# Two-layer cross-attention on one Trainium2 core: the bias rows of the prediction as two groups of 32 rows, one for each half of the tokens

## What is computed

```python
def _L0_xattn_ref(query, key, Wq, bq, Wk, bk, Wv, bv, Wo, bo):
    Q = jnp.einsum('bqd,dh->bqh', query, Wq) + bq
    K = jnp.einsum('bkd,dh->bkh', key, Wk) + bk
    V = jnp.einsum('bkd,dh->bkh', key, Wv) + bv
    scores = jnp.einsum('bqh,bkh->bqk', Q, K) * HIDDEN_DIM ** -0.5
    weights = jax.nn.softmax(scores, axis=-1)
    attended = jnp.einsum('bqk,bkh->bqh', weights, V)
    return query + jnp.einsum('bqh,hd->bqd', attended, Wo) + bo

def _L1_xattn_ref(emb, latent, Wq, bq, Wk, bk, Wv, bv, gamma, beta):
    q = jnp.einsum('bte,ef->btf', emb, Wq) + bq
    k = jnp.einsum('bml,le->bme', latent, Wk) + bk
    v = jnp.einsum('bml,le->bme', latent, Wv) + bv
    w = jnp.einsum('bte,bme->btm', q, k) / jnp.sqrt(E)
    w = jax.nn.softmax(w, axis=1)
    pred = jnp.einsum('btm,bme->bte', w, v)
    x = pred + emb
    mu, var = jnp.mean(x, -1, keepdims=True), jnp.var(x, -1, keepdims=True)
    return (x - mu) * jax.lax.rsqrt(var + EPS) * gamma + beta

x = _L0_xattn_ref(x, ctx_512, ...)       # x: 64 x 256 x 512, ctx: 64 x 256 x 256
x = _L1_xattn_ref(x, ctx_512, ...)
```

## Times and profile of the kernel before

| | |
|---|---|
| median of three runs | 1355.17 us (1355.1, 1355.17, 1359.16) |
| the profiled execution, its own time | 1356.32 us |
| its span in the profile | 1354.3 us |
| PE matmul busy | 1303.7 us, 96% of the span, 9072 matmuls |
| PE weight load busy | 1198.4 us, 88% |
| DVE, ACT, POOL busy | 837.9 us (62%), 769.2 us (57%), 850.3 us (63%) |
| mean granted TensorE clock | 0.992 |
| DMA | 140.56 MB, 104 GB/s on average |

### The profile page before, as it was taken

The page is one execution under the profiler, slowest core; times in us unless marked ns, Lnnn a source line. Parts: engine busy times, 40 slices in busy tenths (PEclk is TensorE's granted clock), DMA queues, the critical chain, the costliest instruction groups (busy, mean ns, idle before and its releaser), DMA issues.

```text
span 1354.3 us, 25114 instructions
## 1 busy us (share of the span) xinstructions
PE 1303.7 (96%) x9072; PEld 1198.4 (88%) x9072; DVE 837.9 (62%) x1682; ACT 769.2 (57%) x1801; POOL 850.3 (63%) x649
## 2 busy tenths in 40 slices
PE   7999999999999999999999999999999999999994
PEld 5789989998998999999999999999899899989983
DVE  1356666666667566666666666756666666666663
ACT  2356566556655655656655665565565665566542
POOL 3246766666666676676666666667667666666744
PEclk8999999999999999999999999999999999999997
DMA  9013323322322322332232232233233233223011
GB/s 365 17 48 123 110 88 114 116 101 93 124 93 93 124 104 83 122 108 89 112 118 98 93 124 93 93 124 105 83 122 108 89 112 119 98 93 124 34 46 46
DMA packets 29558, 140.56 MB, mean 104 GB/s; under 512 B 3680, under 2 KB 3680, under 8 KB 20960
## 3 DMA queue, kind: packets, MB, share of 16 engines
q1 hardware_dynamic: 28656, 139.47, 28.4%
q10 hardware_dynamic: 880, 0.79, 0.2%
HBM read 106.70 MB, written 33.55 MB: 104 GB/s over the span
## 4 chain that ended last, share of the span: by engine, by line
PE 73%; DVE 13%; ACT 9%; issue 3%; DMA 1%; POOL 0%; ACTq 0%; POOLq 0%; DVEq 0%
PE bank L224 62%; PE bank L230 7%; ACT uT_hi L468 4%; DVE nmax L686 3%; DVE bank L683 3%; DVE PcT_lo L619 3%; DVE uT_lo L626 3%; ACT bank L523 2%; ACT PcT_hi L446 2%; PE bank L355 2%; DMA beta_b<-in_beta 1%; PE bank L371 1%; PE bank L365 1%; DVE yT_lo L619 0%; PE bank L384 0%
## 5 line engine op out<-in xcount | busy, mean ns | idle before, releaser
L836 POOL TENSOR_TENSOR dots<-R,g_b 128x512 f32<-128x512 f32 x128 | 165.0, 1290 | 291.6 <-DVE R L661 275.6
L853 POOL TENSOR_TENSOR Y<-Y,gamma_b 128x512 f32<-128x512 f32 x128 | 165.0, 1291 | 159.0 <-ACT Y L552 159.0
L856 POOL TENSOR_TENSOR Y<-Y,beta_b 128x512 f32<-128x512 f32 x128 | 162.7, 1297 | 0.0
L825 POOL TENSOR_TENSOR xT_lo<-IN,xT_hi 128x1024 fp32r<-128x1024 f32 x64 | 154.2, 2410 | 13.0 <-ACT xT_hi L446 13.0
L224 PE MATMUL bank<-xT_hi,A_hi 128*128 128x256 f32 x512 | 155.8, 304 | 0.0
L828 POOL TENSOR_TENSOR CC_lo<-IN,CC_hi 128x1024 fp32r<-128x1024 f32 x64 | 153.9, 2405 | 0.0
L446 ACT ACTIVATE yT_hi<-bank 128x512 fp32r<-128x512 f32 x128 | 69.6, 596 | 141.5 <-PE bank L230 141.5
L224 PE MATMUL bank<-xT_hi,A_lo 128*128 128x256 f32 x512 | 145.1, 283 | 0.0
L224 PE MATMUL bank<-xT_lo,A_hi 128*128 128x256 f32 x512 | 144.5, 282 | 0.0
L661 DVE SCALAR_TENSOR_TENSOR R<-bank,rz,R 128x512 f32<-128x512 f32 x128 | 96.0, 751 | 77.6 <-PE bank L224 77.6
L224 PE MATMUL bank<-yT_hi,A_hi 128*128 128x256 f32 x512 | 143.5, 280 | 0.5 <-DVE yT_lo L619 0.2
(11 more groups left out here) (117 smaller groups left out, 4254.6 us busy)
## 6 DMA issues: line engine op xcount, KB each, us to landing
IN<-in_packed SPq DMA_DIRECT2D x64, 1024.0 KB, 4.8
R<-in_x SPq DMA_DIRECT2D x64, 512.0 KB, 3.3
out<-Y SPq DMA_DIRECT2D x64, 512.0 KB, 2.6
WqT_s<-in_WqT SPq DMA_DIRECT2D x2, 1024.0 KB, 11.2
WkT_s<-in_WkT SPq DMA_DIRECT2D x2, 512.0 KB, 12.2
Wo_s<-in_Wo SPq DMA_DIRECT2D x1, 1024.0 KB, 12.7
WvT_s<-in_WvT SPq DMA_DIRECT2D x1, 512.0 KB, 10.4
Wv_s<-in_Wv SPq DMA_DIRECT2D x1, 512.0 KB, 20.6
```

What stands on the lines that cost most here:

```text
L825: nc.gpsimd.tensor_tensor(flat(xT[n.k % 2][1]), raw[:, 0:XW], fp(flat(xT[n.k % 2][0])), ALU.subtract).then_inc(xT_lo, 1)
L836: nc.gpsimd.tensor_tensor(dots[q][:, :], R[n.k % 4][:, q, :], g1_b[:, :], ALU.mult).then_inc(dot_set, 1)
L853: nc.gpsimd.tensor_tensor(y[:, q, :], y[:, q, :], gamma_b[:, :], ALU.mult).then_inc(Y_mul, 1)
L856: last = nc.gpsimd.tensor_tensor(y[:, q, :], y[:, q, :], beta_b[:, :], ALU.add)
```

## The change

The matmul of 128 rows at the head of each half is gone. In its place each half has a group of five rows in 32 partitions: half 0 in partitions 0 to 31, half 1 in partitions 32 to 63. Two matmuls of 32 contraction rows and 512 columns, one into bank 6 and one into bank 7, stand next to each other in the new function `biases(n)` at the end of PE's body, behind the product of half 1. `pred_full` is now counted by them. The products start their banks themselves.

`pick` has ones in columns 0 to 2 and 32 to 34. A small table `marks`, loaded from memory, makes the five rows of a group: `s_h` writes `s_top`, the rounded sum of `s_bank` and a mark, over 64 rows, and `s_l` writes `srow` as `s_top` times a mark plus `s_bank`, over 64 rows, in place of a subtraction on one row. The rows of a group hold high, low and high of `s`, and two ones; `bvK` holds the same five products as before. On DVE `x2(r-1, 0)` leaves its place and stands directly ahead of `x2(r-2, 1)` at the head of the next body. The small loads are ten in place of seven: one for the marks, four for the rows of `bv1` and `bo0` (10 rows of 2 KB in all, in place of 128), and the rest as before.

```diff
-        bvK = sb("bvK", [P, D], f32r)
-        row = sb("row", [P, D])
-        row_hi = sb("row_hi", [P, D], f32r)
-        less = sb("less", [P, 1])
+        bvK = sb("bvK", [2 * 32, D], f32r)
+        row = sb("row", [2 * 32, D])
+        row_hi = sb("row_hi", [2 * 32, D], f32r)
+        mark = sb("mark", [P, 3])
...
-        srow = sb("srow", [P, S], f32r)
+        s_top = sb("s_top", [2 * 32, S], f32r)
+        srow = sb("srow", [2 * 32, S], f32r)
...
         def _(pe):
-            def product(dst, stat, mov, k, first=True):
+            def product(dst, stat, mov, k, stop=True):
                 for t in range(k):
                     for n, (a, b) in enumerate(((0, 0), (0, 1), (1, 0))):
-                        last = nc.tensor.matmul(dst, stat(a, t), mov(b, t), start=(first and t == 0 and n == 0),
-                                                stop=(t == k - 1 and n == 2))
+                        last = nc.tensor.matmul(dst, stat(a, t), mov(b, t), start=(t == 0 and n == 0),
+                                                stop=(stop and t == k - 1 and n == 2))
                 return last
...
                     pe.wait_ge(x2_set, n.count(2, q, back=1))
-                dst = pred_bank[q][:, :]
-                nc.tensor.matmul(dst, srow[:, q * P:(q + 1) * P], bvK[:, :], start=True, stop=False)
-                product(dst, lambda a, t: wcT[a][:, t, q * P:(q + 1) * P], lambda b, t: V1[b][:, t, :], LT,
-                        first=False).then_inc(pred_full, 1)
+                product(pred_bank[q][:, :], lambda a, t: wcT[a][:, t, q * P:(q + 1) * P], lambda b, t: V1[b][:, t, :], LT,
+                        stop=False)
+
+            def biases(n):
+                if not n.there():
+                    return
+                for k in range(ST):
+                    rows = slice(32 * k, 32 * k + 32)
+                    nc.tensor.matmul(pred_bank[k][:, :], srow[rows, k * P:(k + 1) * P], bvK[rows, :],
+                                     start=False, stop=True).then_inc(pred_full, 1)
...
-            pe.wait_ge(b_in, 16 * 7)
+            pe.wait_ge(b_in, 16 * 10)
...
                 pred_(r.plus(-1), 1)
+                biases(r.plus(-1))
...
                 act.dma_start(bcol[:, n, :], v.rearrange("(p t) -> p t", p=P)).then_inc(b_in, 16)
-            for dst, v in ((row[0:96, :], bv1), (row[96:P, :], bo0), (gamma_b[:, :], gamma), (beta_b[:, :], beta)):
+            act.dma_start(mark[:, :], marks).then_inc(b_in, 16)
+            act.wait_ge(pick_set, 1)
+            for dst, v in ((row[0:3, :], bv1), (row[32:35, :], bv1), (row[3:5, :], bo0), (row[35:37, :], bo0),
+                           (gamma_b[:, :], gamma), (beta_b[:, :], beta)):
                 act.dma_start(dst, v.rearrange("(a n) -> a n", a=1).to_broadcast([dst.shape[0], D])
...
                 act.wait_ge(s_full, n.count())
-                copy(srow[0:96, :], s_bank[0:96, 0:S]).then_inc(s_hi, 1)
+                nc.scalar.activation(s_top[:, :], s_bank[0:64, 0:S], ACT.Identity, bias=mark[0:64, 0:1]
+                                     ).then_inc(s_hi, 1)
...
                 dve.wait_ge(s_hi, n.count())
-                minus(srow[32:33, :], s_bank[32:33, 0:S], srow[32:33, :]).then_inc(s_lo, 1)
+                nc.vector.scalar_tensor_tensor(srow[:, :], fp(s_top[:, :]), mark[0:64, 1:2], s_bank[0:64, 0:S],
+                                               ALU.mult, ALU.add).then_inc(s_lo, 1)
...
-            nc.vector.memset(fp(srow[96:P, :]), 0.0).then_inc(pick_set, 1)
+            nc.vector.memset(row[:, :], 0.0).then_inc(pick_set, 1)
             dve.wait_ge(pick_set, 1)
-            for c in (0, 32, 64):
-                nc.vector.memset(fp(pick[:, c:c + 1]), 1.0)
-            nc.vector.memset(fp(srow[96:98, :]), 1.0).then_inc(pick_set, 1)
+            nc.vector.memset(fp(pick[:, 0:3]), 1.0)
+            nc.vector.memset(fp(pick[:, 32:35]), 1.0).then_inc(pick_set, 1)
...
-            dve.wait_ge(b_in, 16 * 7)
-            nc.vector.tensor_tensor(row[96:P, :], bank[0][96:P, :], row[96:P, :], ALU.add).then_inc(su_lo, 1)
+            dve.wait_ge(b_in, 16 * 10)
+            nc.vector.scalar_tensor_tensor(row[:, :], bank[0][0:64, :], mark[0:64, 0:1], row[:, :], ALU.mult,
+                                           ALU.add).then_inc(su_lo, 1)
             dve.wait_ge(su_hi, 8)
-            dve.wait_ge(const_set, 5)
-            nc.vector.scalar_tensor_tensor(bvK[:, :], fp(row_hi[:, :]), less[:, 0:1], row[:, :], ALU.mult, ALU.add
+            nc.vector.scalar_tensor_tensor(bvK[:, :], fp(row_hi[:, :]), mark[0:64, 2:3], row[:, :], ALU.mult, ALU.add
...
             def body(r):
+                x2(r.plus(-2), 0)
                 x2(r.plus(-2), 1)
...
                 w_l(r)
-                x2(r.plus(-1), 0)
                 yT_l(r.plus(1), 0)
...
-            nc.gpsimd.memset(less[:, :], 0.0).then_inc(const_set, 1)
-            for n, p in enumerate((64, 97)):
-                pool.wait_ge(const_set, 3 + n)
-                nc.gpsimd.affine_select(out=less[:, :], in_=less[:, :], compare_op=ALU.not_equal, fill=-1.0,
-                                        base=-p, pattern=[[0, 1]], channel_multiplier=1).then_inc(const_set, 1)
             split_lo(Seq(0))
             split_lo(Seq(1))
             pool.wait_ge(su_lo, 9)
             dot(Seq(0), 0)
             dot(Seq(0), 1)
             split_lo(Seq(2))
-            pool.wait_ge(b_in, 16 * 7)
+            pool.wait_ge(b_in, 16 * 10)
...
+
+
+    marks = _np.zeros((P, 3), _np.float32)
+    for base in (0, 32):
+        marks[base + 3:base + 5, 0] = 1
+        marks[base + 1, 1], marks[base + 3:base + 5, 1] = -1, 1
+        marks[base + 2, 2], marks[base + 4, 2] = -1, -1
+    arrays["marks"] = marks
```

More of the change, by code:

```diff
@@ L42, in index, with build @@
         return self.k if self.base is None else 4 * self.base + self.k
-def build(nc, x, packed, WqT0, bq0, WkT0, WvT0, bv0, Wo0, bo0, WqT1, WkT1, bk1, Wv1, bv1, gamma, beta, out):
+def build(nc, x, packed, WqT0, bq0, WkT0, WvT0, bv0, Wo0, bo0, WqT1, WkT1, bk1, Wv1, bv1, gamma, beta, marks, out):
     f32, f32r = mybir.dt.float32, mybir.dt.float32r
```

## The result

| | before | changed |
|---|---|---|
| median | 1357.16 us (4 runs, 1355.1 to 1359.37) | 1370.88 us (4 runs, 1369.45 to 1372.68) |
| ratio | | 1.0101, 95% interval 1.0076 to 1.0127 |
| span in the profile | 1354.3 us | 1367.7 us |
| period of the loop | 20.03 us | 20.18 us |
| PE waits ahead of c0 until | 19.51 us | 21.02 us |

A forecast was written before the change was run, and what follows sets the result against it. PE was taken to bound the loop, except for the stretch from u's end to `out_`. Loop -14.3, ends +1.7 and setup 0 summed to -12.6 us, from 1356.3 to 1343.7; range 1340 to 1380.

The forecast's parts named there:

- the first rival: Between product and pair, and pair and S0, the array empties at 0.28 us each: 1379.6 us; chance 0.30.
- the price of the pair: On PE at the body's end, 0.23 us for both matmuls against 0.46 removed: -0.23 a body, -14.3 us in all.
- The sign that the prediction named for being wrong: On PE, the pair taking over 0.4 us from the product's last slot to S0; a period above 20.1 means the drain.
- Its point of decision: Around the pair, emptying the array decides the result from 0.135 us a change on, where the loss passes 4 us.
- Its case of half the price: Around the pair, the array empties at half of 0.28 us a change: 1364 us, included in the chance of 0.30.
- The argument against this rival: On PE, weight loads run ahead under matmuls throughout, also where shapes change, which spoke against the array emptying.
- the second rival: Around the pair, no drain but uncovered weight loads: pair 0.41 us, 1355.1; or no sharing, 1358; chance 0.20 together.
- The x2 move: On DVE, max0 comes 1.07 us later, ACT keeps about 0.13 in hand, and the loop pays nothing.
- The rival of ACT as the bound: In the loop, x2 0.4 us later delays uT_hi by some 0.27 a body: 1360 us; chance 0.04.
- srow: ACT's write of 64 rows costs nothing more; DVE's new two-input operation takes about 0.48 us and fits in 3.2.
- The ends: In the last two sequences nothing covers the later x2 on DVE: +0.85 us each, together +1.7.
- The setup: Ahead of c0, PE's wait for the small loads: taken as 0, with -2.3 and +2 us as ends.

The follow-up runs named there:

- run 2: Changed kernel with both 32-row bias matmuls reading the same rows 0 to 31, so that they can't share the array: 1386.14 us, ratio 1.0209.
- run 4: Changed kernel with the pair of bias matmuls issued twice in a row: 1386.51 us, ratio 1.0213.
- run 3: Changed kernel's data, each 32-row bias matmul alone ahead of its half's product, x2 in its old place: 1410.01 us, ratio 1.0386.
- E0: Not a run: a tile whose transposes on PE, first (sequence 0) to last (sequence 63), measure the loop: 1265.2 us before, 1275.7 changed.
- run 1: Kernel before, with its two 128-row bias matmuls moved to the body's end and the first x2 moved as in the change: 1359.7 us, ratio 1.0017.
- run 6: Changed kernel with the pair between the transposes and the product of half 1, x2 in its old place: 1369.48 us, ratio 1.0095.
- run 7: Kernel before, with half of the next sequence's S0 moved behind wc_, ahead of out_, where PE stood still: 1324.38 us, ratio 0.9766.
- run 5: Changed kernel with the two groups of 64 rows, at partitions 0 and 64, instead of 32: 1369.92 us, ratio 1.0096.

## Why the prediction was wrong

The sign and the size were wrong: 1343.7 was forecast, 1370.88 came. The stated range, up to 1380, holds it only because it was drawn to include the first rival.

**The step that failed** is the price of the pair: "I take 0.23, because the nearest rows, neighbours that change bank, tile and width (657.33 to 657.57), show no cost of a change." None of those rows changes the number of contraction rows, so they were no evidence about it. The pair costs 0.47 + 0.15 = 0.62: 0.23 for two matmuls that do share (runs 2 and 4), and 0.2 for each of two changes (runs 3 and 4). In the sum that term was -14.3 us; the loop gave +10.5 by the transposes of E0. The sign that the prediction named for being wrong came: from the product's last slot to S0 it is 0.51 us (663.14 + 0.23 to 663.88), over its 0.4, and the period is 20.18, over its 20.1.

**The first rival** had the place and the kind of the cost. It named the two places, between the product and the pair and between the pair and S0, and said that the array empties there. It priced a change at 0.28, from 0.17 of running out and 0.11 of a restart; measured are 0.19 to 0.20. Its point of decision, 0.135, lay below. With 0.20 its own working gives 0.23 + 0.40 - 0.47 = 0.16 a body, times 62 about +10, and with the ends 1368 to 1369. Its case of half the price is written as 1364; by the same working, 0.23 + 0.28 - 0.46 = 0.05 a body, it is about 1362. The argument against this rival, that weight loads run ahead "throughout", was a wrong reading too: behind the transposes they did not (655.81 and 655.84). The rule of the Trainium skill that the prediction quoted, in TensorEngine Tiling (Array Packing), section Key Properties, that a change of mode drains TensorE, fits every run here: each change costs 0.19 to 0.20 us. The other rule, of the Trainium skill's TensorE: Matmul & The Clock Gate, Part 3: Packing small matmuls, that a group in different rows takes one matmul and a few nanoseconds, agrees: the pair's merged row is 0.49 us long, and a second pair costs 0.23 (run 4). Both are true at once, and only their sum decides.

What the runs show is the time of the change and that weight loads don't run ahead across it. That the array empties inside is the reading that fits; no view shows the inside, and no run separates emptying from late weight loads. Late loads alone, the second rival's 0.09 each, are too little: the pair would cost 0.41 and costs 0.62.

**The x2 move**: right. Forecast were max0 3.1 us behind S0, and an ACT with about 0.13 in hand; it came at 2.97, the second normalisation ended at 671.82, 0.13 ahead of uT_hi, which stayed released by PE, and runs 1 and 6 show the loop untouched. The rival of ACT as the bound did not come.

**srow**: right in effect. DVE's operation took the 0.47 that its bound allowed. ACT's was said to cost nothing more; it takes 0.46 (676.45) and took 0.38 as a copy of more rows. Nobody waits for it.

**The ends**: +1.7 forecast. From the last transposes of E0 to the end of the span it is 53.4 us, 1.4 longer than before, and the last x2 starts 1.34 behind its twin, as forecast. That the sum is close is partly luck: of the last sequence's matmuls ten ran at a granted clock of 0.50 (4.40 us) where seven had before (3.13 us), at a slot of 0.43 instead of 0.23, which makes about 0.6 of the 1.4.

**The setup**: taken as 0 between -2.3 and +2, measured +1.5 (21.02 against 19.51 at c0). Fewer bytes didn't help. The load that PE waited for last, that of beta, left ACT later, because three more were issued ahead of it; before and changed:

```profile
3.88 0.51 ACTq L451 DMA_DIRECT2D beta_b<-in_beta  x1
```

```profile
4.94 0.47 ACTq L462 DMA_DIRECT2D beta_b<-in_beta  x1
```

That is 1.06 of the 1.51 us. From the issue to c0 it is 16.08 us instead of 15.63, the other 0.45; how much of that the marks and how much the short rows make was not tried.

The pieces add up: 1.5 in the setup, 10.5 in the loop and 1.4 at the end make the 13.4 us between the spans. They must, since they are cuts of the same two spans; what each is made of was shown above.

## What to carry to other kernels

Packing small matmuls side by side pays only when the group saves more than its two borders cost: here 0.4 us for both, against 0.23 for each full matmul of 512 columns that is saved. By these prices a shared group that stands for two full matmuls loses, and one that stands for three about breaks even (an estimate from 3 x 0.23 against 0.23 + 0.40, if a third shares as the second does; no run tried three). When no row of the trace shows an operation, rows that differ in another respect are not its price; the likeliest value then belongs where a mechanism puts it. And a busy share of 96% hid a stop of 0.55 us in each body: 0.71 us of work whose inputs were ready, moved there from the next body, filled it and gave back 32 us (run 7), more than twice the 14.3 us that sharing promised.

## What the runs showed of the hardware that was not expected

- A change between 128 and 32 or 64 contraction rows costs PE 0.19 to 0.20 us, in and out alike, at a granted clock of 1.00, with 512 columns ahead and 256 or 512 behind, and with transposes or products beside it (runs 3 to 6).
- At such a border weight loads start with their matmul (663.46), inside a product a slot ahead of it (662.91). They also start with it behind the transposes (655.81 and 655.84), where no rows change and the slot is 0.32; there, too, the way in costs 0.18 (run 6). So how much of the price is the late load is open.
- ACT's activation Identity with a bias from a column took 0.46 us on 64 x 256, its Copy 0.38 on 96 x 256.
- A wait of PE of 4.26 us in the setup was followed by a stretch at the lower clock level, granted 0.50 from 24 to 28 us; taking the wait away brought c0 3.6 us forward and the first transposes of E0 6.8 us.
